# Row gathers by the sync and scalar queues: addresses as register pairs, more rows by hand, node tiles loaded singly

## Chip, core and metric

The kernel runs on one core of one Trainium2 chip. The metric is the device time of one execution in microseconds (us), as the median of several runs of the same program.

## What is computed

One layer of a graph network on 12,500 nodes with 256 features each and 200,000 edges that are sorted by their target node:

```python
h = jnp.maximum(_layernorm(x, axis=-1), 0.0)
agg = jax.ops.segment_sum(h[src], dst, num_segments=N)
z = (1.0 + eps_gin) * h + agg
t = jnp.dot(z, W1) + b1                       # 256 -> 512
t = jax.nn.relu(_batchnorm(t, g1, bt1))       # over all nodes
conv_out = jnp.dot(t, W2) + b2                # 512 -> 256
out = x + jax.nn.relu(_batchnorm(conv_out + h, g2, bt2))
```

## The kernel before, in words

**Tiles and groups.** The edges are cut into 1,563 tiles of 128 edges, the tiles into 196 groups of 8 (the last has 3). For a tile the 128 source rows of 1 KB each are fetched into SBUF, one row to a partition. TensorE multiplies them by a 128 x 96 selection matrix that VectorE makes from the target numbers, and sums the 8 tiles of a group in PSUM into a window of 96 target nodes (`aggregate`, L1324). The window is copied out, transposed (L1334) and added to `aggT` (L840). TensorE's loop has one step to a group. Every second step also brings in a node tile (128 rows of h itself, `transpose_h`, L1351), and four node tiles make a chunk that goes through W1 (`times_W1`, L1360). The chunk's result `t` is written to DRAM by `store_t` (L476). Node tile c is transposed in TensorE's step 2c + 7.

**Two phases.** Groups 0 to 29 fetch rows of x and normalise them after the fetch, since h isn't complete yet. Beside this ScalarE and VectorE normalise all of x in batches and store it as `h_rows` in DRAM. `wait_h` lets a queue go on when the last batches have landed. From group 30 on the rows are fetched from `h_rows` and used as they are; ScalarE then has no arithmetic after its step 33 until the last groups, and issues row fetches only.

**Who fetches.** Most tiles are fetched by GpSimd, with one indirect DMA of 128 rows a tile (`gather`, L650). The buffers hold four groups: group g may be fetched once group g - 4 is aggregated. Some tiles are fetched by hand, row by row: SyncE takes the last tile of the groups in `sp_groups`, ScalarE the last but one of those in `act_groups`, each with `load_rows`. A row costs a plain DMA of 1 KB whose source offset is a register. The registers are filled 32 at a time by a register load (`reg_load`, L505 on SyncE, L1191 on ScalarE) from a line of row offsets that was fetched from DRAM before (`load_at`). 16 rows are a piece, 8 pieces a tile, and each of the two engines has three row buffers: tile j may be begun when tile j - 3 has been used. GpSimd leaves these tiles out.

**How many.** `SP_EIGHTHS` counts eighths of a piece that SyncE takes in a pass. SyncE's loop has one pass for each node tile, that is for two groups, and 12 eighths are 1.5 pieces or 24 rows a pass. `ACT_EIGHTHS` counts in the same way for each of ScalarE's steps, that is for one group: 7 eighths are 14 rows. The lists of groups follow from these numbers, as in

```python
while True:
    done = ceil(8 * per_tile * (len(act_groups) + 1), ACT_EIGHTHS) + H_ACT
    if done - 1 + 4 >= NG - 4:
        break
    act_groups.append(done - 1 + 4)
```

They give SyncE 16 tiles (2 of them rows of x) and ScalarE 17, and leave 1,530 to GpSimd.

**The order on SyncE.** A pass issues, in order: the node tile's load (L460 in the first phase; in the second `load_quad`, L467, which loads four node tiles in one DMA in every fourth pass, after a wait until the four tiles that were in that buffer are transposed), every fourth pass `store_t` (it waits until the chunk's t is complete), then the rows of the pass. A DMA on this queue is issued only after all that stand before it.

Of the kernel before, what the change touches and what calls it, by code (L numbers as in the profile page):

```python
# [20 lines left out]
P = 128  # L21
D = 256
F = 512
DB, FB = D // P, F // P
GT = 8
# [11 lines left out]
XW = Q * D  # L37
X_FIRST = 4
X_EARLY = 16
SP_EIGHTHS = 12  # L40
ACT_EIGHTHS = 7
H_FROM = 30
H_NODES = 14
HB = 4
# [4 lines left out]
ROW_BUFS = 3  # L49
PIECE = 16  # L50
AT_ONCE = 32
QUAD = 4
ROW_BYTES = 4 * D


# [4 lines left out]
def build(nc, x, src, dst, W1, b1, g1, bt1, W2, b2, g2, bt2, eps_gin, out):  # L60
# [4 lines left out]
    N, E = x.shape[0], src.shape[0]  # L65

    NI = ceil(E, P * SLOTS)
    NT = ceil(N, P)
    assert NI == NT and NI >= 4 and N % 4 == 0 and NI * PG <= BANK
    LASTN = N - P * (NT - 1)  # L70
# [15 lines left out]
    with ctx:  # L86
# [3 lines left out]
        def sem(name):  # L90
            return ctx.enter_context(nc.semaphore(name))
# [4 lines left out]
        h_dram = nc.dram_tensor("h_rows", (N, D), f32, kind="Internal").ap()  # L96
# [8 lines left out]
        while True:  # L105
            done = ceil(8 * per_tile * (len(sp_groups) + 1), SP_EIGHTHS)
            if done > H_NODES or 2 * (done - 1) + 6 >= H_FROM:
# [3 lines left out]
        while True:  # L111
            done = ceil(8 * per_tile * (len(sp_groups) - SP_X + 1), SP_EIGHTHS) + H_NODES
            if 2 * (done - 1) + 6 >= NG - 4:
# [4 lines left out]
# [3 lines that stand above are left out]
# [22 lines left out]
        work, once, tables, ring = (arena[:, sum(MAIN[:n]):sum(MAIN[:n + 1])] for n in range(4))  # L143
# [6 lines left out]
                 work[:, 2 * GT * D:3 * GT * D])]  # L150
        hb = [a[:, n * 4 * D:(n + 1) * 4 * D].rearrange("p (j d) -> p j d", d=D) for a in
              (ring[:, 2 * GT * D:3 * GT * D], work[:, 2 * GT * D:3 * GT * D]) for n in (0, 1)]
        quads = [ring[:, 2 * GT * D + n * QUAD * D:2 * GT * D + (n + 1) * QUAD * D].rearrange("p (j d) -> p j d", d=D)
                 for n in (0, 1)]
        assert (NT - H_NODES) % QUAD == 0 and 2 * QUAD == GT
        after_rows = [work[:, 3 * GT * D + n * D:3 * GT * D + (n + 1) * D] for n in range(4)]
        tab_i = [work[:, n * EB * P:(n + 1) * EB * P].bitcast(i32).rearrange("p (b e) -> p b e", e=P) for n in (0, 1)]
        tab_f = [work[:, (2 + n) * EB * P:(3 + n) * EB * P].rearrange("p (b e) -> p b e", e=P) for n in (0, 1)]
# [42 lines left out]
        hx = after_rows[3]  # L201
# [68 lines left out]
        s_bn, s_mv, s_sd, s_rstd, s_st, s_h, s_sel, s_agg, s_add = (  # L270
            sem(n) for n in ("s_bn", "s_mv", "s_sd", "s_rstd", "s_st", "s_h", "s_sel", "s_agg", "s_add"))
        s_xt = [sem("s_xt_even"), sem("s_xt_odd")]
        s_quad = [sem("s_quad_even"), sem("s_quad_odd")]
        s_ev, s_wT = sem("s_ev"), sem("s_wT")
        s_xbn, s_xmv, s_xsd, s_xrs, s_xst, s_hx, s_hT, s_hTc, s_zt, s_t, s_tb, s_tst, s_td = (
            sem(n) for n in ("s_xbn", "s_xmv", "s_xsd", "s_xrs", "s_xst", "s_hx", "s_hT", "s_hTc", "s_zt",
                             "s_t", "s_tb", "s_tst", "s_td"))
# [67 lines left out]

            return a[b * QN + 4 * first:b * QN + 4 * end, :].rearrange("(p j) d -> p j d", j=4)

        NQUAD = (NT - H_NODES) // QUAD

        def quad_count(k):  # L350

            return 16 * (k // 2 + 1 + (k == NQUAD - 1))

        def quad_tile(c):

            k, j = divmod(c - H_NODES, QUAD)
            return quads[k % 2][:, j, :]

        def wait_h(eng):

# [67 lines left out]
        def _(sp):  # L428
# [7 lines left out]
            for n, a in ((1, dst), (0, src)):  # L436
                at = FULLB * P * P
# [8 lines left out]
            for a in (b1, g1, bt1, b2, g2, bt2):  # L446
                k = a.shape[0] // P
# [11 lines left out]
                    sp.wait_ge(s_hx, c - 1)  # L459
                sp.dma_start(xt[c % 2][0:n, :], x[bass.ds(c * P, n), :]).then_inc(s_xt[c % 2], 16)  # L460

            def load_quad(k):
                if k >= 2:
                    sp.wait_ge(s_hT, H_NODES + QUAD * (k - 1))
                first = H_NODES + QUAD * k
                n = QUAD if k < NQUAD - 1 else QUAD - 1
                sp.dma_start(quads[k % 2][:, 0:n, :],  # L467
                             h_dram[first * P:(first + n) * P, :].rearrange("(j p) d -> p j d", p=P)
                             ).then_inc(s_quad[k % 2], 16)
                if n < QUAD:  # L470
                    sp.dma_start(quad_tile(NT - 1)[0:LASTN, :], h_dram[N - LASTN:N, :]).then_inc(s_quad[k % 2], 16)

            def store_t(q):
                sp.wait_ge(s_tb, FB * (q + 1))
# [21 lines left out]
            def load_rows(j, m):  # L496
                if m == 0:
                    if j + 1 < len(sp_groups):
                        load_at(j + 1)
                    if j >= ROW_BUFS:  # L500
                        sp.wait_ge(s_agg, sp_groups[j - ROW_BUFS] + 1)
                    sp.wait_ge(s_spat[j % 2], 16 * (j // 2 + 1))
                if m * PIECE % AT_ONCE == 0:
                    regs = [sp.alloc_register(f"row{j}_{m}_{k}") for k in range(AT_ONCE)]
                    sp.reg_load(regs, sp_at[j % 2][0:1, m * PIECE:m * PIECE + AT_ONCE])  # L505
                    row_regs.extend(regs)
                for k in range(PIECE):
                    e = m * PIECE + k
                    reg = row_regs.pop(0)
                    at = sp.snap(reg, donate=True, min_val=0, max_val=(N - 1) * ROW_BYTES)  # L510
                    a = x_bytes if j < SP_X else h_bytes
                    sp.dma_start(sp_rows[j % ROW_BUFS][e:e + 1, :].bitcast(mybir.dt.uint8),
                                 a[bass.ds(at, ROW_BYTES)].rearrange("(p e) -> p e", p=1)
                                 ).then_inc(s_sprows[j % ROW_BUFS], 16)
                    sp.free_register(reg)

            sp.wait_ge(s_at, 1)
            sp.dma_start(at_dram.rearrange("b p e -> p b e"), tab_i[0]).then_inc(s_atd, 16)
            def pieces_of_pass(c):
# [16 lines left out]
            for c in range(NT):  # L536
                if c == NT - 1:
                    store_t(NQF - 2)
                if c < H_NODES:
                    load_node_tile(c)  # L540
                elif c == H_NODES:
                    wait_h(sp)
                    load_quad(0)
                    load_quad(1)
                elif (c - H_NODES) % QUAD == 2 and (c - H_NODES) // QUAD + 2 < NQUAD + 1:
                    k = (c - H_NODES) // QUAD + 1
                    if k >= 2:
                        load_quad(k)
                if 2 * Q < c < NT - 1 and c % Q == 1:
                    q = (c - 2 * Q - 1) // Q  # L550
                    if q == NQF - 3:
                        sp.wait_ge(s_td, 16 * q)
                        load_t(0, 0, 0)
                    store_t(q)
                if c == 0:
                    sp.wait_ge(s_trc[0], NTR)
                    sp.wait_ge(s_trc[1], NTR)
                    for b in (2, 3):
                        sp.dma_start(hb[b], batch_nodes(x, b, 0, P)).then_inc(s_pl[b], 16)
                    sp.wait_ge(s_atd, 16)  # L560
                    load_at(0)
                for j, m in pieces_of_pass(c):
                    load_rows(j, m)
# [47 lines left out]
            q, n = last_order(NQ - 1)  # L611
# [455 lines left out]
        def _(act):  # L1067
# [114 lines left out]
            def load_rows(j, m):  # L1182
                if m == 0:
                    if j + 1 < len(act_groups):
                        load_at(j + 1)
                    if j >= ROW_BUFS:
                        act.wait_ge(s_agg, act_groups[j - ROW_BUFS] + 1)
                    act.wait_ge(s_actat[j % 2], 16 * (j // 2 + 1))
                if m * PIECE % AT_ONCE == 0:
                    regs = [act.alloc_register(f"act_row{j}_{m}_{k}") for k in range(AT_ONCE)]  # L1190
                    act.reg_load(regs, act_at[j % 2][0:1, m * PIECE:m * PIECE + AT_ONCE])  # L1191
                    row_regs.extend(regs)
                for k in range(PIECE):
                    e = m * PIECE + k
                    reg = row_regs.pop(0)
                    at = act.snap(reg, donate=True, min_val=0, max_val=(N - 1) * ROW_BYTES)
                    act.dma_start(act_rows[j % ROW_BUFS][e:e + 1, :].bitcast(mybir.dt.uint8),
                                  h_bytes[bass.ds(at, ROW_BYTES)].rearrange("(p e) -> p e", p=1)
                                  ).then_inc(s_actrows[j % ROW_BUFS], 16)
                    act.free_register(reg)  # L1200
            act.wait_ge(s_atd, 16)
            load_at(0)

# [33 lines left out]
            a, c, q = NG - 4, NT - 4, NQF - 2  # L1237
# [52 lines left out]
        def _(pe):  # L1290
# [46 lines left out]
            def transpose_h(c):  # L1337
                n = P if c < NT - 1 else LASTN
                if c < H_NODES:
                    pe.wait_ge(s_hx, c + 1)  # L1340
                else:
                    k = (c - H_NODES) // QUAD
                    pe.wait_ge(s_quad[k % 2], quad_count(k))
                h = hx if c < H_NODES else quad_tile(c)
                if 1 <= c < NT - 1:
                    pe.wait_ge(s_hTc, c)
                if c == NT - 1:
                    pe.wait_ge(s_sel, NG)
                hT = hT_ps if c < NT - 1 else hT_last
                for f in range(DB):  # L1350
                    last = T.transpose(hT[:, f, 0:n], h[0:n, f * P:(f + 1) * P], ident[0:n, 0:n])  # L1351
                last.then_inc(s_hT, 1)
# [40 lines left out]
            a, c, q = NG - 4, NT - 4, NQF - 2  # L1393
# [90 lines left out]
```

## Time and profile before

| | |
|---|---|
| median of 3 runs | 2143.56 us (2143.31 to 2145.06) |
| the profiled execution: its own time | 2143.43 us |
| its span in the profile | 2141.6 us |
| GpSimd gathers (L650) | 16 + 222 + 1292 = 1530 |
| GpSimd issues gathers from / to | 3.8 us / 1916.5 us |
| granted TensorE clock, mean | 0.83 |

The span is the time from the first to the last instruction that the profiler saw. Times of single instructions are in ns, stretches in us from the span's start. PE is TensorE, DVE is VectorE, ACT is ScalarE, POOL is GpSimd, SP is SyncE; SPq and ACTq are the DMA issues of these engines. Register loads and moves and DMA issues are not counted as busy time of an engine.

### The profile page before, as it was taken

How to read it: one execution, taken by the hardware profiler on the slowest of the kernel's cores; microseconds unless marked ns; L12 is line 12 of the kernel's file. 1: busy time of each engine (PE TensorE's matmuls, PEld its weight loads, DVE VectorE, ACT ScalarE, POOL GpSimd, SP SyncE). 2: the span in 40 equal slices, each digit the busy share in tenths (PEclk: the TensorE clock that was granted, in tenths of full speed). 3: DMA queues.
4: the chain of work that ended last, by engine and by line, in shares of the span. 5: the costliest groups of instructions: out<-in, count | busy, mean ns of one | idle time of the engine just before them, and what ended most of it. 6: DMA issues, size and time to landing. Idle time of an engine off the chain costs nothing.

```text
span 2141.6 us, 24025 instructions
## 1 busy us (share of the span) xinstructions
PE 1430.6 (67%) x4835; PEld 911.2 (43%) x4835; DVE 768.3 (36%) x1947; ACT 338.3 (16%) x661; POOL 1449.2 (68%) x1540
## 2 busy tenths in 40 slices
PE   3656666665655766675666566666666666689998
PEld 2434344443433434343444334434344444454446
DVE  7777753222322222322232222222232232234447
ACT  6767660000000000000000000000000000014446
POOL 7777777777777777777777777777777777760000
PEclk7788788877888787888888887778787788899999
DMA  6666654444434434444444443443443444448438
GB/s 200 214 224 218 225 175 129 132 117 139 138 108 139 138 110 136 137 118 130 136 126 119 138 139 108 138 137 107 140 137 108 136 135 123 137 133 321 176 135 319
DMA packets 123554, 325.22 MB, mean 152 GB/s; under 512 B 32179, under 2 KB 55294, under 8 KB 117266
## 3 DMA queue, kind: packets, MB, share of 16 engines
q0 software_dynamic: 73440, 200.64, 32.0%
q1 hardware_dynamic: 39100, 97.34, 12.8%
q10 hardware_dynamic: 10870, 25.75, 3.6%
q8 instruction: 38, 0.62, 0.1%
q14 instruction: 106, 0.87, 0.1%
HBM read 271.55 MB, written 52.05 MB: 151 GB/s over the span
## 4 chain that ended last, share of the span: by engine, by line
POOL 65%; issue 21%; PE 12%; DMA 2%; ACT 0%; DVE 0%; SPq 0%; POOLq 0%; DVEq 0%
POOL arena L650 65%; PE ps L1442 8%; PE ps L1324 2%; PE ps L1456 2%; DMA arena<-h_rows,arena 1%; PE ps L1360 0%; PE ps L1398 0%; DMA arena<-in_src 0%; ACT aggT L1072 0%; SPq L439 0%; ACT arena L1078 0%; ACT arena L1076 0%; DVE arena L1057 0%; PE ps L1334 0%; SPq L433 0%
## 5 line engine op out<-in xcount | busy, mean ns | idle before, releaser
L650 POOL DMA_INDIRECT arena<-h_rows,arena x1292 | 1221.6, 946 | 394.0 <-issue 391.5
L1324 PE MATMUL ps<-arena 128*96 128x256 f32 x3060 | 976.9, 489 | 675.2 <-DMA arena<-h_rows,arena 561.5
L1324 PEld LDWEIGHTS ps<-arena 128*96 128x96 f32 x3060 | 640.8, 216 | 993.3 <-issue 732.4
L840 DVE TENSOR_TENSOR aggT<-aggT,ps 128x192 f32 x196 | 69.3, 353 | 1074.2 <-PE ps L1334 1071.2
L1151 ACT COPY arena<-ps 96x256 f32<-96x256 f32 x37 | 13.2, 357 | 1575.5 <-PE ps L1334 1545.0
L650 POOL DMA_INDIRECT arena<-in_x,arena x222 | 209.9, 946 | 67.7 <-issue 67.7
L1360 PE MATMUL ps<-arena 128*128 128x512 f32 (+3 forms) x412 | 186.3, 577 | 1.6 <-DVE arena L873 1.5
L1442 PE MATMUL ps<-arena,W2s 128*128 128x512 f32 (+1 forms) x400 | 168.1, 582 | 0.9 <-ACT arena L1272 0.8
L927 DVE TENSOR_TENSOR arena<-arena,ps 128x768 f32<-128x768 f32 x159 | 149.8, 942 | 0.0
L1103 ACT ACTIVATE arena<-arena,nb,mv 128x256 f32<-128x256 f32 x238 | 120.2, 587 | 83.6 <-DVE nb L744 81.5
L1442 PEld LDWEIGHTS ps<-arena,W2s 128*128 128x128 f32 x400 | 75.7, 190 | 93.2 <-issue 86.3
L676 DVE BATCH_NORM_STATS2 st<-arena 128x6 f32<-128x256 f32 x238 | 80.5, 410 | 61.5 <-DMA arena<-in_x,arena 61.4
L1360 PEld LDWEIGHTS ps<-arena 128*128 128x128 f32 x412 | 69.7, 190 | 48.1 <-issue 44.5
L1272 ACT ACTIVATE arena<-arena,sh,sc 128x512 f32<-128x512 f32 (+1 forms) x100 | 72.1, 792 | 90.2 <-PE ps L1442 80.3
L924 DVE TENSOR_SCALAR arena<-ps,prmT 128x512 f32<-128x512 f32 x79 | 59.3, 751 | 73.7 <-PE ps L1360 73.7
L1035 DVE SCALAR_TENSOR_TENSOR aggT<-ps,prmT,aggT 128x512 f32<-128x512 f32 (+1 forms) x50 | 36.9, 738 | 95.7 <-PE ps L1442 95.7
L881 DVE BATCH_NORM_STATS2 arena<-arena 128x6 f32<-128x512 f32 x92 | 62.9, 684 | 10.3 <-ACT arena L1160 10.3
L1334 PEld LDWEIGHTS ps<-ident,arena 96*128 96x128 f32 x392 | 55.3, 142 | 26.5 <-ACT arena L1151 1.2
L918 DVE COPY arena<-ps 96x256 f32<-96x256 f32 x159 | 65.8, 414 | 0.1
L1334 PE MATMUL ps<-ident,arena 96*128 96x96 f32 x392 | 64.9, 246 | 0.6 <-ACT arena L1151 0.5
L1117 ACT ACTIVATE arena<-arena,pnb,pmv 128x256 f32<-128x256 f32 (+1 forms) x100 | 51.7, 591 | 0.0
L756 DVE TENSOR_TENSOR arena<-arena,ps 128x768 f32<-128x768 f32 x37 | 35.0, 945 | 8.7 <-PE ps L1324 8.7
(99 smaller groups left out, 575.2 us busy)
## 6 DMA issues: line engine op xcount, KB each, us to landing
W2s<-h_rows ACTq DMA_DIRECT2D x2176, 1.0 KB
rl_odd<-h_rows SPq DMA_DIRECT2D x1792, 1.0 KB
t_T<-arena SPq DMA_DIRECT2D x24, 1024.0 KB, 4.9
arena<-t_T SPq DMA_DIRECT2D x24, 1024.0 KB, 4.8
arena<-h_rows,arena POOLq DMA_INDIRECT x1292, 2.8
arena<-in_x SPq DMA_DIRECT2D x27, 512.0 KB, 5.7
h_rows<-arena ACTq DMA_DIRECT2D x24, 512.0 KB, 3.4
out<-arena SPq DMA_DIRECT2D x23, 512.0 KB
```

The source lines that it names most:

```text
L650: nc.gpsimd.indirect_dma_start(out=rows[slot(g)][:, k, :], out_offset=None, in_=(x if g < H_FROM else h_dram)[:, :], in_offset=bass.Indire ...
L676: last = V.bn_stats(o, r)
L840: V.tensor_tensor(z, z, winT_ps, ALU.add).then_inc(s_add, 1)
L881: V.bn_stats(o, t[:, m, :]).then_inc(s_tst, 1)
L918: V.tensor_copy(win_sb[g % 2], win_ps[g % 2]).then_inc(s_ev, 1)
L927: V.tensor_tensor(sel[:, g % 2, :, :], rel[:, g * GT:(g + 1) * GT].unsqueeze(2).to_broadcast([P, GT, W]), iota_ps.unsqueeze(1).to_broadcas ...
L1103: last = S.activation(rows_of(g, k), rows_of(g, k), ACT.Relu, bias=nb[:, g % 2, k:k + 1], scale=mv[:, g % 2, k, 1:2])
L1272: S.activation(u[:, k % 2, f, 0:n], tin[:, k % 2, f, 0:n], ACT.Relu, bias=sh1[:, f:f + 1], scale=sc1[:, f:f + 1]).then_inc(s_u, 1)
L1324: last = T.matmul(win_ps[g % 2], sel[:, g % 2, k, :], rows_of(g, k), start=k == 0, stop=k == n - 1)
L1334: last = T.transpose(winT_ps[:, f, :], win_sb[w % 2][:, f * P:(f + 1) * P], ident[0:W, 0:W])
L1360: last = T.matmul(t_ps[(FB * q + m) % TB][:, a:b], W1s[:, k, m * P:(m + 1) * P], zt[q % 2][:, k, a:b], start=k == 0, stop=k == DB - 1)
L1442: last = T.matmul(c_ps[k % 2][m][:, 0:n], W2s[:, f, m * P:(m + 1) * P], u[:, k % 2, f, 0:n], start=f == 0, stop=f == FB - 1)
```

## The change

Three things change together. The row's address is given as a pair of registers, the offset and a register that holds zero for the upper half, in place of the offset alone. SyncE takes 44 rows a pass in place of 24, ScalarE 22 rows a group in place of 14. And in the second phase each node tile is loaded by a DMA of its own, three passes ahead (four in pass 14), into a ring of eight buffers, in place of four tiles in a DMA.

```diff
-SP_EIGHTHS = 12
-ACT_EIGHTHS = 7
+SP_EIGHTHS = 22
+ACT_EIGHTHS = 11
...
-QUAD = 4
+NODE_BUFS = 8
+NODES_AHEAD = 4
...
-            def load_quad(k):
-                if k >= 2:
-                    sp.wait_ge(s_hT, H_NODES + QUAD * (k - 1))
-                first = H_NODES + QUAD * k
-                n = QUAD if k < NQUAD - 1 else QUAD - 1
-                sp.dma_start(quads[k % 2][:, 0:n, :],
-                             h_dram[first * P:(first + n) * P, :].rearrange("(j p) d -> p j d", p=P)
-                             ).then_inc(s_quad[k % 2], 16)
...
+            def load_node_rows(c):
+                n = P if c < NT - 1 else LASTN
+                if c - NODE_BUFS >= H_NODES:
+                    sp.wait_ge(s_hT, c - NODE_BUFS + 1)
+                sp.dma_start(node_tile(c)[0:n, :], h_dram[c * P:c * P + n, :]
+                             ).then_inc(s_node[(c - H_NODES) % NODE_BUFS], 16)
...
-                    at = sp.snap(reg, donate=True, min_val=0, max_val=(N - 1) * ROW_BYTES)
+                    at = sp.snap(bass.Register64Pair(reg, no_high), donate=True, min_val=0,
+                                 max_val=(N - 1) * ROW_BYTES)
...
+            no_high = sp.alloc_register("no_high")
+            sp.reg_mov(no_high, 0)
...
                 elif c == H_NODES:
                     wait_h(sp)
-                    load_quad(0)
-                    load_quad(1)
-                elif (c - H_NODES) % QUAD == 2 and (c - H_NODES) // QUAD + 2 < NQUAD + 1:
-                    k = (c - H_NODES) // QUAD + 1
-                    if k >= 2:
-                        load_quad(k)
+                    for n in range(NODES_AHEAD):
+                        load_node_rows(c + n)
+                elif c + NODES_AHEAD - 1 < NT:
+                    load_node_rows(c + NODES_AHEAD - 1)
...
-                    at = act.snap(reg, donate=True, min_val=0, max_val=(N - 1) * ROW_BYTES)
+                    at = act.snap(bass.Register64Pair(reg, no_high), donate=True, min_val=0,
+                                 max_val=(N - 1) * ROW_BYTES)
```

TensorE's `transpose_h` waits for the node tile's own semaphore in place of the quad's.

## Rows read from the trace of the kernel before

**Rows 1.** The page: busy time by engine (GpSimd's line), and the chain that ended last.

```profile
PE 1430.6 (67%) x4835; PEld 911.2 (43%) x4835; DVE 768.3 (36%) x1947; ACT 338.3 (16%) x661; POOL 1449.2 (68%) x1540
POOL 65%; issue 21%; PE 12%; DMA 2%; ACT 0%; DVE 0%; SPq 0%; POOLq 0%; DVEq 0%
```

**Rows 2.** Groups of instructions: busy us, mean ns of one, idle before with its releasers.

```profile
L650 POOL DMA_INDIRECT arena<-h_rows,arena x1292 | 1221.6, 946 | 394.0 <-issue 391.5 <-PE ps L1324 2.4
L1324 PE MATMUL ps<-arena 128*96 128x256 f32 x3060 | 976.9, 489 | 675.2 <-DMA arena<-h_rows,arena 561.5 <-ACT arena L1103 101.0 <-ACT rl_odd L1103 6.8
```

**Rows 3.** Line L650 over the span: ns min/median/max, first and last start.

```profile
L650 POOL DMA_INDIRECT arena<-h_rows,arena x1292: 942/946/1005, 302.2 to 1916.5; - x185
L650 POOL DMA_INDIRECT arena<-in_x,arena x222: 942/946/969, 24.6 to 300.9; - x111
```

**Rows 4.** Row issues and register loads, by line: ns min/median/max.

```profile
L512 SPq MOVE rl_odd<-h_rows x1792: 29/29/29, 298.7 to 1742.0; - x200
L512 SPq DMA_DIRECT2D rl_odd<-h_rows x1792: 227/228/532, 298.8 to 1742.1; - x200
...
L1197 ACTq DMA_DIRECT2D W2s<-h_rows x2176: 234/235/1232, 316.6 to 1638.8; - x198
...
L505 SPq TENSOR_LOAD <-rl_odd x64: 2032/2132/4272, 24.5 to 1699.7; - x64
...
L1191 ACTq TENSOR_LOAD <-W2s x68: 2136/2245/4123, 314.3 to 1626.1; - x68
```

**Rows 5.** Timeline of SyncE's queue, 950 to 1050 us: start, length, what.

```profile
957.79 0.40 SPq L467 DMA_DIRECT2D arena<-h_rows  x1
...
964.29 0.36 SPq L476 DMA_DIRECT2D t_T<-arena  x1
...
994.75 5.17 SPq L512 DMA_DIRECT2D rl_odd<-h_rows  x16
1035.39 0.41 SPq L467 DMA_DIRECT2D arena<-h_rows  x1
```

**Rows 6.** Timeline of SyncE's queue at the start: two issues without a move between.

```profile
7.42 0.25 SPq L448 DMA_DIRECT2D arena<-in_L_gnn_b  x1
7.72 0.25 SPq L448 DMA_DIRECT2D arena<-in_L_gnn_g  x1
```

**Rows 7.** Timeline of ScalarE's queue, 870 to 1012 us.

```profile
876.29 51.64 ACTq L1197 DMA_DIRECT2D W2s<-h_rows  x128
...
963.84 48.27 ACTq L1197 DMA_DIRECT2D W2s<-h_rows  x118
```

**Rows 8.** Waits of SyncE's queue: us in total, times, longest.

```profile
SPq L467 <- PE ps L1351: 630.7, 19, 64.0
SPq L476 <- DVE arena L924: 126.5, 20, 20.2
```

**Rows 9.** DMA queues, 1065 to 1083 us: packets, MB, share of 16 engines.

```profile
q0 software_dynamic: 678, 1.86, 36.5%
q1 hardware_dynamic: 87, 0.05, 1.1%
q10 hardware_dynamic: 89, 0.05, 1.0%
...
W2s<-h_rows ACTq DMA_DIRECT2D x48, 1.0 KB
```

**Rows 10.** Line L650, 1065 to 1083 us.

```profile
L650 POOL DMA_INDIRECT arena<-h_rows,arena x15: 942/946/949, 1065.0 to 1082.5; - x15
```

**Rows 11.** Timeline of TensorE after the change of phase.

```profile
318.15 3.67 PE L1324 MATMUL ps<-arena 128*96 128x256 f32 x16
...
343.89 3.66 PE L1324 MATMUL ps<-arena 128*96 128x256 f32 x16 [2.33 <-DMA arena<-h_rows,arena]
```

**Rows 12.** Timeline of SyncE's queue in the first phase.

```profile
61.49 0.37 SPq L460 DMA_DIRECT2D arena<-in_x  x1
61.95 14.53 SPq L512 DMA_DIRECT2D rl_odd<-in_x  x32
```

More of the change, by code:

```diff
@@ L152, in build @@
               (ring[:, 2 * GT * D:3 * GT * D], work[:, 2 * GT * D:3 * GT * D]) for n in (0, 1)]
-        quads = [ring[:, 2 * GT * D + n * QUAD * D:2 * GT * D + (n + 1) * QUAD * D].rearrange("p (j d) -> p j d", d=D)
-                 for n in (0, 1)]
-        assert (NT - H_NODES) % QUAD == 0 and 2 * QUAD == GT
+        node_rows = ring[:, 2 * GT * D:3 * GT * D].rearrange("p (j d) -> p j d", d=D)
+        assert NODE_BUFS == GT
         after_rows = [work[:, 3 * GT * D + n * D:3 * GT * D + (n + 1) * D] for n in range(4)]
@@ L272, in build @@
         s_xt = [sem("s_xt_even"), sem("s_xt_odd")]
-        s_quad = [sem("s_quad_even"), sem("s_quad_odd")]
+        s_node = [sem(f"s_node{b}") for b in range(NODE_BUFS)]
         s_ev, s_wT = sem("s_ev"), sem("s_wT")
@@ L346, in batch_nodes, with node_tile, node_count @@
             return a[b * QN + 4 * first:b * QN + 4 * end, :].rearrange("(p j) d -> p j d", j=4)
[L348 to L357, printed above, removed]
+        def node_tile(c):
+            return node_rows[:, (c - H_NODES) % NODE_BUFS, :]
+        def node_count(c):
+            return 16 * ((c - H_NODES) // NODE_BUFS + 1)
         def wait_h(eng):
@@ L460, in load_node_tile @@
                 sp.dma_start(xt[c % 2][0:n, :], x[bass.ds(c * P, n), :]).then_inc(s_xt[c % 2], 16)
-            def load_quad(k):
-                if k >= 2:
-                    sp.wait_ge(s_hT, H_NODES + QUAD * (k - 1))
-                first = H_NODES + QUAD * k
-                n = QUAD if k < NQUAD - 1 else QUAD - 1
-                sp.dma_start(quads[k % 2][:, 0:n, :],
-                             h_dram[first * P:(first + n) * P, :].rearrange("(j p) d -> p j d", p=P)
-                             ).then_inc(s_quad[k % 2], 16)
-                if n < QUAD:
-                    sp.dma_start(quad_tile(NT - 1)[0:LASTN, :], h_dram[N - LASTN:N, :]).then_inc(s_quad[k % 2], 16)
+            def load_node_rows(c):
[4 more added lines that the diff above has]
+                             ).then_inc(s_node[(c - H_NODES) % NODE_BUFS], 16)
             def store_t(q):
@@ L1200, in load_rows @@
                     act.free_register(reg)
+            no_high = act.alloc_register("act_no_high")
+            act.reg_mov(no_high, 0)
             act.wait_ge(s_atd, 16)
@@ L1341, in transpose_h @@
                 else:
-                    k = (c - H_NODES) // QUAD
-                    pe.wait_ge(s_quad[k % 2], quad_count(k))
-                h = hx if c < H_NODES else quad_tile(c)
+                    pe.wait_ge(s_node[(c - H_NODES) % NODE_BUFS], node_count(c))
+                h = hx if c < H_NODES else node_tile(c)
                 if 1 <= c < NT - 1:
```

## The prediction

> **What bounds the kernel now.** I read the page first. No engine is busy for more than 68% of the span, so the shares alone don't name a bound. The chain that ended last does: 65% of the span is GpSimd's gather line and 21% is "issue", which is GpSimd's own gap between two gathers [rows 1]. The reader is to see that these two are one thing. The groups of instructions confirm it: before its 1,292 gathers of h rows GpSimd idles 394.0 us, and all but 2.4 us of that is "issue", not a wait for anybody [rows 2]. TensorE on its side idles 675.2 us before the aggregation, and 561.5 us of it end with the landing of a gather [rows 2]. So GpSimd never waits, and the others wait for it.
>
> Its pace comes from first and last starts. From 302.2 to 1916.5 us lie 1,291 intervals, 1614.3 / 1291 = 1.250 us each; from 24.6 to 300.9 us lie 221, again 1.250 us [rows 3]. A gather costs 1.25 us in both phases, with everything that happens beside it. The time before the first gather and the work after the last are not touched by the change.
>
> **What the change takes off GpSimd.** The lists of groups follow from the two numbers. SyncE's h tiles end in pass 14 + ceil(64 n / 22) and so on up to the last group below 192; I count 4 tiles of x (2 before) and 27 of h (14 before), the last for group 190. ScalarE gets 27 (17 before), the last also for group 190. That is 58 tiles in place of 33, so GpSimd keeps 1,505 of 1,563: 25 fewer, 2 of them in the first phase. 25 x 1.250 = 31.3 us. This is the whole gain if SyncE and ScalarE have their rows ready in time and GpSimd keeps its pace. The rest of this part is about that "if".
>
> **What a row costs the issuing queues.** Today a row is a move of 29 ns and a DMA issue of 228 ns on SyncE (235 ns on ScalarE) [rows 4]. Sixteen rows take 5.17 us from the first start to the last end, so a period is (5.17 - 0.23) / 15 = 0.33 us, 0.322 if the first, slower one is left out; 0.322 - 0.228 - 0.029 leaves 0.065 us for two gaps [rows 4, 5]. The move fills the upper half of the address. I take it that the pair does away with it, which saves 0.029 + 0.032 = 0.061 us: 0.261 us a row on SyncE and 0.264 on ScalarE. The bounds: nothing saved (0.322), if a second issue must follow the first no sooner than now. The nearest rows without a move between are two small loads at the start, 0.30 us from start to start with 0.25 us of issue [rows 6]; by their gap of 0.05 a row would take 0.28. I stay with 0.261, as the row's own issue and gap are seen 1,792 times.
>
> **ScalarE's budget.** A tile of 128 rows takes it 51.64 us [rows 7] plus the register load ahead of the first row, 2.25 us [rows 4]: 53.9 us with all its loads. Less 128 x 0.061 = 7.8 it is 46.1 us. After the change a group of the second phase has 8 - 2 x 22/128 = 7.66 gathers, 9.57 us, and ScalarE must deliver a tile in 128/22 = 5.82 groups, 55.7 us. It has 9.6 us to spare, and still 1.8 us if nothing is saved.
>
> **SyncE's budget.** Four passes take it from 957.79 to 994.75 + 5.17 = 999.92, 42.1 us, for 96 rows, one quad, one `store_t` and three register loads, one of them right behind the store [rows 5]. Afterwards four passes hold 176 rows: 80 more are 25.8 us at today's period, 2.5 more register loads of 2.13 us [rows 4] are 5.3, three more node loads of 0.41 us and a gap [rows 5] 1.4, the more frequent row-offset loads 0.2; the saved moves give back 176 x 0.061 = 10.7. Sum 64.1 us, 16.0 a pass. Four passes of GpSimd are 8 x 9.57 = 76.6 us. Spare: 12.5 us, or 1.8 if nothing is saved.
>
> **The node tiles.** Today SyncE waits 630.7 us in 19 quad loads, up to 64.0 us each [rows 8]: it does four passes in 42 us, then stands until four node tiles are used. With 64 us of work in each 76.6 these bursts would leave little cover; loading singly, a pass c waits only for tile c - 5 to be transposed, so SyncE may run five passes ahead. What holds it then is `store_t`, which waits for t today too (126.5 us in 20 waits, [rows 8]): it can be issued in TensorE's step 8q + 18 for chunk q, and VectorE needs it done by step 8q + 23. SyncE arrives there ahead, so nothing behind it is late: the rows queued behind the store are due at step 8q + 24. I cost the ring at nothing; the cover is these five steps, some 48 us. Without it each late microsecond would be one of the end.
>
> **The first phase.** SyncE's first tile is now for group 10, in passes 0 to 2. Pass 1 starts at 61.5 us, and 32 rows of x took it 14.5 us [rows 12]. With 48 rows in it and in pass 2 the tile is issued by about 61.5 + 19 + 18 = 99 us. GpSimd's seventh gather of group 10 is the 71st of those that start at 24.6 us, thus at 24.6 + 70 x 1.25 = 112 us [rows 3]. Cost nothing, cover 13 us.
>
> **The change of phase.** In its steps 29 to 32 ScalarE has row pieces ahead of its window copies: 5 in place of 3, with one more register load. 32 x 0.264 + 2.2 - 48 x 0.061 = 7.7 us later. TensorE has a backlog there: from 318.15 to 343.89 us it goes through four groups in 25.7 us and only then waits for a gather again [rows 11], where GpSimd needs 40 us for four. The 14 us hide the 7.7. Without this cover they would be added whole.
>
> **DMA engines.** With both row streams running beside GpSimd, its own queue takes 36.5% of 16 engines, the rows 1.1% and 1.0% for 43 and 45 rows in 18 us [rows 9]. The worst case is that all rows go through one engine. It then spends 2.1% x 16 = 34% on them, 36.5% on gathers, 70% in all; at 0.26 us a row 34 becomes 42, together 78%. So no engine is full. GpSimd's gathers in that stretch still start 17.5 / 14 = 1.25 us apart [rows 10]. [...]
>
> **Sum.** 2143.43 - 31.3 = 2112.2 us against the profiled execution's own time; the median is 0.13 above that, so 2112.3.
>
> **The rivals.**
> *Start-up leaks.* The 7.7 us of the change of phase reach GpSimd through its four group buffers: 2112.3 + 7.7 = 2120. Against it the backlog above; for it that the buffers' slack in the first phase is under a group. 6%.
> *Rows become the bound (the other side).* If the pair costs a second move instead of saving one, a row on ScalarE takes 0.386 us and a tile 53.9 + 7.8 = 61.7. ScalarE starts at about 310 us (316.6 today, [rows 4], with a piece in one step earlier) and would end 27 tiles at 310 + 27 x 61.7 = 1976. Group 190's gathers are issued today 43 gathers before the last, by 1916.5 - 53.8 = 1862.7. So 113 us slower: 2257. It turns slower than before once a tile costs over (1862.7 - 310) / 27 = 57.5 us, a row over 0.264 + 11.4 / 128 = 0.353. For it: I haven't seen the instructions of a pair. Against: only a rise over today's 0.325 can do it. 4%.
> *Issues take turns.* SyncE's and ScalarE's issues could exclude one another, 0.228 + 0.235 = 0.463 us for a pair of rows. Then four passes of SyncE take 64.1 + 176 x 0.202 = 99.7 us, 27 tiles of 2.91 passes end at 299 + 78.5 x 24.9 = 2254, 391 us past 1862.7: 2535. Against it: 43 + 45 rows went out in 18 us beside register loads, where turns allow 39 pairs [rows 9], and both medians are those of a lone issue [rows 4]. 1%. The Trainium skill ("Perfetto Trace Analysis", section "DMA Instruction — HWDGE (DVE, Sync)") has the rule: a descriptor generator shared by the sequencers and locked by one at a time. The trace doesn't agree at this rate.
> *GpSimd slows down.* More row traffic lengthens each gather. Break-even is 31.3 / 1505 = 21 ns, 1.271 us a gather; half of that gives 2128. Against it the equal pace in both phases and in rows 10. 4%.
> *The pair saves nothing.* Both budgets keep 1.8 us: still 2112, part of the forecast.
>
> **How the numbers follow.** The forecast has 85%, with its own range 2110 to 2116. The range to state reaches below to 2109 (half a gather's noise and a slightly earlier start of phase two) and above over the start-up case and small losses, to 2122; what lies outside is the row bound, the turns and a slowed GpSimd, about 1 in 10. A change under 0.2% (4.3 us) can't be told from none. Faster: forecast, start-up and half of the slowed-GpSimd case, 0.92. Same 0.03, slower 0.05.
>
> **What would show it.** In the profile after: 1,505 gathers, still 946 ns and 1.25 us apart; the last one starts near 1916.5 - 31.3 = 1885 us; no MOVE at the row line and 16 rows in about 4.2 us; ScalarE's 128 rows in 44 us; quad waits of 630 us gone, a few waits of `load_node_rows` and longer ones of `store_t` in their place; TensorE waits for gathers, not for `rl_odd` or `W2s` rows. Wrong would be: GpSimd waiting for TensorE over more than some us, TensorE's idle time ended by row DMAs, or gathers further apart.

## The result: slower by 1.1%, and the profile after

The changed kernel takes 2167.77 us (2166.18 to 2169.39) against 2143.43 us in the same comparison: ratio 1.0112, 95% interval 1.0095 to 1.013. The forecast was 2112.3 us. The span of the profiled execution is 2165.6 us (2141.6 before).

The gathers first, line L644 of the changed kernel; they answer to [rows 2] and [rows 3].

```profile
L644 POOL DMA_INDIRECT arena<-h_rows,arena x1269: 942/946/963, 300.2 to 1940.3; - x182
L644 POOL DMA_INDIRECT arena<-in_x,arena x220: 942/946/957, 24.2 to 299.0; - x110
```

With 16 more at the start there are 1,505 of them, each still 946 ns. The last one starts at 1940.3 us, where the forecast had 1885: 55 us late, and 55 us are all that is missing (2167.8 - 2112.3). The waits of the changed kernel say why (engine, line, what it waited for; us in total, times, longest):

```profile
POOL arena L644 <- issue: 452.8, 1484, 0.3
PE ps L1321 <- DMA arena<-h_rows,arena: 321.4, 74, 9.0
DVE arena L918 <- DMA t_T<-arena: 279.8, 15, 37.2
PE ps L1321 <- DMA rl_odd<-h_rows: 174.2, 15, 21.6
...
PE ps L1321 <- DVE arena L921: 88.4, 9, 24.0
...
POOL arena L644 <- PE ps L1321: 60.8, 18, 9.1
```

GpSimd now waits 60.8 us for TensorE to free its buffers, where it waited 2.4 before. TensorE waits 174.2 us for `rl_odd`, which is SyncE's rows, and VectorE 279.8 us for the store of t, which stands in the same queue. That second wait reaches TensorE too: it waits 88.4 us for the selection matrices (L921), which VectorE makes behind the copy that the store holds up; in the kernel before this was 1.5 us. ScalarE's rows (`W2s`) end none of these waits. The chain that ended last has changed hands; the issues of SyncE's queue, 0% of it in [rows 1], are now 35%:

```profile
SPq 35%; POOL 29%; issue 17%; PE 14%; DMA 3%; DVE 0%; ACT 0%; DVEq 0%; POOLq 0%
```

So SyncE's queue is late. Its row line, to be read against [rows 4], and its waits against [rows 8]:

```profile
L506 SPq MOVE rl_odd<-h_rows x3456: 29/29/29, 298.4 to 1893.9; - x192
L506 SPq DMA_DIRECT2D rl_odd<-h_rows x3456: 227/228/2461, 298.5 to 1893.9; - x192
```

```profile
SPq L469 <- ACT arena L1154: 27.9, 1, 27.9
...
SPq L469 <- DVE arena L918: 3.7, 2, 3.1
```

Two things stand there. The move of 29 ns is still in front of each of the 3,456 rows. And the longest issue is 2,461 ns where it was 532, though the median is the same 228. SyncE itself hardly waits any more: for t 3.7 us in place of 126.5, and once, after 1800 us, 27.9 us for the last t that ScalarE makes (73.7 before); there are no quad waits. The timeline of its queue over four passes answers to [rows 5]:

```profile
1424.65 0.48 SPq L463 DMA_DIRECT2D arena<-h_rows  x1
1425.19 0.42 SPq L469 DMA_DIRECT2D t_T<-arena  x1
1425.71 7.32 SPq L506 DMA_DIRECT2D rl_odd<-h_rows  x16
...
1467.73 18.86 SPq L506 DMA_DIRECT2D rl_odd<-h_rows  x48
...
1487.10 5.64 SPq L506 DMA_DIRECT2D rl_odd<-h_rows  x16
...
1507.67 0.36 SPq L463 DMA_DIRECT2D arena<-h_rows  x1
```

From node load to node load these are 1507.67 - 1424.65 = 83.0 us for four passes without a wait, where GpSimd needs 76.6. Sixteen rows take 5.64 to 7.32 us here, 5.17 in [rows 5]. Over the 14 such stretches between 502 and 1671 us the mean is 83.5.

### The profile page after: what moved, and what is told of

Same layout as the page of the kernel before. It is cut to its first block, busy times and chain, and to the rows that moved or that the text cites. A ratio compares the mean times of both kernels' runs of the same rounds, so it can differ in the third digit from the quotient of the medians.

```text
span 2165.6 us, 30624 instructions
## 1 busy us (share of the span) xinstructions
PE 1367.9 (63%) x4835; PEld 882.2 (41%) x4835; DVE 765.9 (35%) x1947; ACT 338.5 (16%) x661; POOL 1425.0 (66%) x1515
## 4 chain that ended last, share of the span: by engine, by line
SPq 35%; POOL 29%; issue 17%; PE 14%; DMA 3%; DVE 0%; ACT 0%; DVEq 0%; POOLq 0%
POOL arena L644 29%; SPq L506 28%; PE ps L1438 8%; SPq L498 6%; PE ps L1321 3%; DMA rl_odd<-h_rows 2%; PE ps L1452 1%; DMA arena<-h_rows,arena 1%; PE ps L1356 1%; SPq L463 1%; SPq L485 0%; SPq L469 0%; PE ps L1394 0%; ACT arena L1097 0%; PE ps L1331 0%
## 5 line engine op out<-in xcount | busy, mean ns | idle before, releaser
L644 POOL DMA_INDIRECT arena<-h_rows,arena x1269 | 1199.7, 945 | 441.6 <-issue 382.0
L1321 PE MATMUL ps<-arena 128*96 128x256 f32 x3010 | 909.0, 468 | 760.4 <-DMA arena<-h_rows,arena 321.4
L1321 PEld LDWEIGHTS ps<-arena 128*96 128x96 f32 x3010 | 603.2, 206 | 1041.3 <-issue 800.1
L644 POOL DMA_INDIRECT arena<-in_x,arena x220 | 208.0, 945 | 68.0 <-issue 66.8
L918 DVE TENSOR_SCALAR arena<-ps,prmT 128x512 f32<-128x512 f32 x79 | 59.1, 749 | 328.4 <-DMA t_T<-arena 279.8
L921 DVE TENSOR_TENSOR arena<-arena,ps 128x768 f32<-128x768 f32 x159 | 149.7, 942 | 0.0
L1438 PEld LDWEIGHTS ps<-arena,W2s 128*128 128x128 f32 x400 | 75.8, 190 | 93.1 <-issue 86.2
L1347 PE MATMUL ps<-ident,arena 128*128 128x128 f32 x196 | 37.3, 272 | 2.3 <-ACT aggT L1138 2.3
```

The source lines that it names most:

```text
L644: nc.gpsimd.indirect_dma_start(out=rows[slot(g)][:, k, :], out_offset=None, in_=(x if g < H_FROM else h_dram)[:, :], in_offset=bass.Indire ...
L921: V.tensor_tensor(sel[:, g % 2, :, :], rel[:, g * GT:(g + 1) * GT].unsqueeze(2).to_broadcast([P, GT, W]), iota_ps.unsqueeze(1).to_broadcas ...
L1321: last = T.matmul(win_ps[g % 2], sel[:, g % 2, k, :], rows_of(g, k), start=k == 0, stop=k == n - 1)
L1438: last = T.matmul(c_ps[k % 2][m][:, 0:n], W2s[:, f, m * P:(m + 1) * P], u[:, k % 2, f, 0:n], start=f == 0, stop=f == FB - 1)
```

## The experiments

Theory A: the rows of both queues overfill something that they share, a DMA engine. Theory B: SyncE simply has too much work of its own. Theory C: the address pairs or the single node loads did it. The runs came in series, each with the kernel before beside it. In four series that kernel took 2570 to 2611 us; their times stand in the last part. The kernel with other row shapes ran in one of those four, which is said there. In the other series the kernel before took 2143.8 to 2144.0 us.

**The counts of before, the rest of the change kept.**

```diff
-SP_EIGHTHS = 22
-ACT_EIGHTHS = 11
+SP_EIGHTHS = 12
+ACT_EIGHTHS = 7
```

> The changed kernel with the row counts of before (12 and 7 eighths): only the address pairs and the node tiles loaded one by one remain of the change. GpSimd has 1,530 gathers again. Theory A (one DMA engine or the issue path is overfilled by rows) and theory B (SyncE alone has more work than a pass of GpSimd's lasts) both expect 2143 us, within 0.2%, as 52 rows a pass leave room in either. If the single node loads themselves are the cause (63 more DMAs in SyncE's queue, theory C), it is slower than before by over 0.2%. The move of 29 ns in front of each row should still be there, as in the changed kernel.

Measured: 2143.40 us, ratio 1.000 (0.999 to 1.001). The pairs and the single loads together cost and bring nothing at these counts. The pair doesn't take the move away:

```profile
L506 SPq MOVE rl_odd<-h_rows x1792: 29/29/29, 299.7 to 1709.9; - x200
```

**One queue's rows as after, the other's as before** (12 and 11 eighths, then 22 and 7).

> The changed kernel with SyncE's rows as before (12 eighths, 24 rows a pass) and ScalarE's as after (11 eighths, 44 rows a pass): 68 rows in two groups in place of 88, 1,520 gathers. If nothing binds but GpSimd: 2143.4 - 10 x 1.25 = 2130.9. Theory A expects about that, 2130 to 2134, with ScalarE's row issues near 235 ns, since the rows of both queues together are 23% fewer. Theory B expects the same. A theory that ScalarE's rows are the late ones expects over 2140.

Measured: 2131.23 us, ratio 0.9941 (0.9925 to 0.9958).

> The changed kernel with SyncE's rows as after (22 eighths, 44 a pass) and ScalarE's as before (7 eighths, 28 a pass): 72 rows in two groups, 1,515 gathers. If nothing binds but GpSimd: 2143.4 - 15 x 1.25 = 2124.7. Theory A (what the two queues share is full) expects 2124 to 2130 and SyncE's mean row issue back from 273 to under 240 ns, since ScalarE's part is smaller. Theory B (SyncE's own work, whatever ScalarE does) expects SyncE to be as late as in the changed kernel: row issues of 270 ns and a time of 2155 to 2168.

Measured: 2125.89 us, ratio 0.9914 (0.9898 to 0.9931). Theory B falls: the same 44 rows a pass are in time when ScalarE issues 28 beside them and not when it issues 44. Four passes of SyncE in this run:

```profile
1419.80 0.36 SPq L463 DMA_DIRECT2D arena<-h_rows  x1
1422.80 0.35 SPq L469 DMA_DIRECT2D t_T<-arena  x1
1427.71 17.70 SPq L506 DMA_DIRECT2D rl_odd<-h_rows  x48
...
1497.76 0.36 SPq L463 DMA_DIRECT2D arena<-h_rows  x1
```

78.0 us, and 2.6 of them are a wait for t ahead of the store: 75.4 us of work. In the changed kernel the same rows, node loads and store take 83.0, although only five register loads (10.4 us) fall into them and six here (14.6 us, one of them behind the store). The row issues make the difference: 230 ns each in this stretch, 294 in the changed kernel's. A run of 48 rows with one register load is 17.70 us here, 18.86 above, and up to 22.02 elsewhere in the changed kernel:

```profile
1095.94 22.02 SPq L506 DMA_DIRECT2D rl_odd<-h_rows  x48
```

**A row's cost by itself.** A kernel that leaves the whole layer out, copies x to the output and issues rows with constant addresses.

```python
for e in range(R):                                        # R = 256, on ScalarE and on SyncE
    act.dma_start(place(act_rows, e), row(e, 1)).then_inc(s_a[1], 16)
act.wait_ge(s_a[1], FULL)
```

> Not the layer: the output is a copy of x, and beside it rows of x are fetched to measure what a row costs. Addresses are constants, so no move and no register load stand between issues. Stage 1: ScalarE alone 256 rows. Stage 2: both queues 256 each. Stage 3: the same beside 48 gathers of GpSimd. Stages 4 and 5: as 2 and 3, but each row cut into 16 pieces of 64 bytes. Theory A with all rows on one DMA engine: stage 1 is issue bound, 0.26 us a row; stage 2 is bound by the engine, 512 rows in 512 x c us, where the changed kernel suggests c of 0.12 to 0.14 us: 61 to 72 us, against 68 us of pure issue, and the issues stretch beyond 235 ns once some 30 rows a queue are outstanding; stage 3 takes about 1/(1 - 0.37) as long, 100 to 115 us. If the cost is a fixed one per row and engine, the cut rows of stages 4 and 5 take as long as the whole ones or longer; if it is bytes, they take less. Theory B expects stages 2 and 3 to stay at 0.26 us a row and queue, 68 us each. GpSimd's gathers should stay 1.25 us apart in stage 3 by both.

Three of its five stages: ScalarE alone issues 256 rows, then both queues 256 each, then both again, with 48 gathers of GpSimd beside the first 60 us. The timeline of both queues, and behind it SyncE's waits for the landing after stages 2 and 3:

```profile
42.80 75.96 ACTq L42 DMA_DIRECT2D act_rows<-in_x  x256
119.77 77.81 ACTq L45 DMA_DIRECT2D act_rows<-in_x  x256
119.83 77.93 SPq L73 DMA_DIRECT2D sp_rows<-in_x  x256
211.97 85.09 SPq L77 DMA_DIRECT2D sp_rows<-in_x  x256
212.03 85.16 ACTq L49 DMA_DIRECT2D act_rows<-in_x  x256
```

```profile
SPq L80 <- DMA act_rows<-in_x: 17.2, 1, 17.2
...
SPq L75 <- DMA act_rows<-in_x: 14.0, 1, 14.0
```

Alone a row takes 75.96 / 256 = 0.297 us to issue, without any move. Two queues issue as fast (0.304), so they don't take turns. But the rows don't land as fast: 77.9 + 14.0 = 91.9 us for 512 rows, 0.180 us each, and 85.1 + 17.2 = 102.3 us, 0.200 each, in the stage with gathers. Theory A expected 61 to 72 us for the first, so a row costs more than the 0.12 to 0.14 us it supposed; the second lies in its 100 to 115. Theory B had 68 us for each. GpSimd's gathers stayed 1.25 us apart. The DMA queues of stage 2, 120 to 197 us (packets, MB, share of 16 engines):

```profile
q1 hardware_dynamic: 440, 0.23, 3.2%
q10 hardware_dynamic: 441, 0.23, 3.0%
```

In stage 1 ScalarE's rows landed as fast as they were issued: to the last one a row's packet started 0.6 to 0.7 us after its issue. In stage 2 that delay grew to 11.7 us. So both queues share something that lets a row pass every 0.18 us. That it is one DMA engine fits but isn't shown by the packets' time: 6.2% of 16 engines is 99% of one, but with rows of 256 bytes (next part) the same sum is 9.8%, or 157% of one, so a packet's time holds some waiting too. What speaks for one engine is the count of packets. A row goes out as one piece and leaves two, one of 1 KB and one of 4 bytes (440 for 220 rows); a row in 16 pieces leaves 16 of each. The Trainium skill ("DMA: Bandwidth & Descriptors", section "Why a DMA increments its semaphore by 16 and not by 1") says that the outermost dimension above 1, as the instruction carries it, decides how many engines a DMA uses, that a [1, 1] scalar uses one, that on these two queues it is always the lowest-numbered ones, and that each engine taking part writes once to the semaphore. The trace agrees with the count; which engine it is can't be seen. Beside gathers, 213 to 272 us:

```profile
q0 software_dynamic: 2193, 5.99, 36.6%
q1 hardware_dynamic: 293, 0.15, 1.6%
q10 hardware_dynamic: 293, 0.15, 1.3%
```

That is 293 rows in 59 us, two packets each, 0.201 us a row: the limit next to gathers, though by packet time the engine would be only 36.6 + 2.9 x 16 = 83% busy. So the packets' time is no measure of what a row costs: too little here, too much at 256 bytes. Stages 4 and 5, with the row cut into 16 pieces that lie together, came out like 2 and 3 (77.95 and 84.37 us of issue) and still sent two packets a row, so the cut had been merged and says nothing.

**Does the size of a row matter?** The same kind of kernel, layer left out, both queues issuing 256 DMAs in each of five stages: whole rows, 256 bytes of each, rows in 4 and in 16 pieces, and two rows (2 KB) in one DMA. It ran in a series where the kernel before took 2611 us; its first stage repeats the 77.9 us of the row kernel, so its issues were not slowed.

```diff
+act.dma_start(whole(act_rows, e, D // 4), row(e, 1, D // 4)).then_inc(s_a[1], 16)      # 256 bytes
+act.dma_start(apart(act_rows, e, 4), pieces(e, 2, 4)).then_inc(s_a[2], 16)             # 4 pieces apart
+act.dma_start(apart(act_rows, e, 16), pieces(e, 3, 16)).then_inc(s_a[3], 16)           # 16 pieces apart
```

> Not the layer: the output is a copy of x. Five stages, in each both queues fetch 256 rows at once with constant addresses and wait until all have landed. Stage 1: whole rows of 1 KB, as measured before, 0.175 us a row from first issue to last packet (89.5 us for 512). Stage 2: 256 bytes of each row. Stage 3: a row in 4 pieces of 256 bytes that don't lie together in SBUF, stage 4 in 16 pieces of 64 bytes, stage 5: two rows, 2 KB, in one DMA. Fixed cost per DMA on its engine: stage 2 and 5 take 85 to 95 us as well, and stages 3 and 4 too, as each engine that takes part pays it. Cost by bytes: stage 2 becomes issue bound (76 us), stage 5 takes 130 us or more, stages 3 and 4 become issue bound as the load is spread over 4 and 16 engines.

The timeline of SyncE's queue, by stage:

```profile
42.62 77.92 SPq L71 DMA_DIRECT2D sp_rows<-in_x  x256
136.54 76.07 SPq L75 DMA_DIRECT2D sp_rows<-in_x  x256
229.77 187.93 SPq L79 DMA_DIRECT2D sp_rows<-in_x  x256
419.51 164.70 SPq L83 DMA_DIRECT2D sp_rows<-in_x  x256
585.45 80.06 SPq L87 DMA_DIRECT2D sp_rows<-in_x  x256
```

With the waits for the landing behind them (15.9, 17.0, 1.7, 0.9 and 14.2 us) 512 DMAs take 93.8 us at 1 KB, 93.1 at 256 bytes and 94.3 at 2 KB. The cost is fixed per DMA, 0.18 us, as expected. The forms in pieces were expected at 85 to 95 us if each engine pays, and missed that: they do not queue up, but their issue takes 0.73 and 0.64 us, far over the 0.30 of a whole row, so cutting a row into pieces is no way out. The DMA queues at 256 bytes, 137 to 226 us:

```profile
q10 hardware_dynamic: 512, 0.07, 6.8%
q1 hardware_dynamic: 512, 0.07, 3.0%
```

**Between the two counts** (18 and 10 eighths, 20 and 10, 20 and 11).

> The changed kernel with 18 and 10 eighths, 76 rows in two groups, 1,514 gathers. 2123.4 if nothing but GpSimd binds, and Theory A expects 2123 to 2125, row issues of SyncE under 245 ns. An effect in proportion to the row count would give about 2155.

> The changed kernel with 20 and 10 eighths, 80 rows in two groups, 1,512 gathers. 2120.9 if nothing but GpSimd binds. Theory A: 80 x 0.204 + 1 = 17.3 us in 19.2, 90% full, so 2121 to 2124, the fastest of this series or level with 84 rows.

> The changed kernel with 20 and 11 eighths, 84 rows in two groups, 1,509 gathers. 2117.2 if nothing but GpSimd binds. Theory A: 17.1 + 1 us of work for the row engine in 19.2 us, 95% full: 2117 to 2130; at such a load the queues behind it should be long (row issues over 240 ns in the mean).

Measured: 2124.51 us (ratio 0.9904, 0.9887 to 0.992), 2120.97 (0.989, 0.9873 to 0.9906) and 2117.89 (0.9875, 0.9859 to 0.9891). All three stand within 1.1 us of what GpSimd's gathers alone give; only the guess that 80 rows would be the fastest or level was off. The last is the fastest version found, 26 us faster than before and 50 faster than the changed kernel. GpSimd waits for TensorE 2.7 us or less in each. The step from 84 to 88 rows, all four of them SyncE's, costs 50 us.

**The same 84 rows, but more of them on SyncE** (22 and 10 eighths).

> The changed kernel with 22 and 10 eighths for the third time, again because the chip before took 2600 us for the kernel before. Theory A (the number of rows on the one engine decides): 2116 to 2119, like 20 and 11. Theory D (SyncE's own work and what its issues lose to the full engine, together): 2135 to 2160.

Measured: 2127.95 us, ratio 0.9924 (0.9907 to 0.9941). This lies between the two expectations: 12 us over the 2115.9 of its gathers, where 20 and 11 is 0.7 over. The total number of rows alone (theory A) doesn't decide; SyncE's own 44 rows do count. Theory D, both together (SyncE's own work and what its issues lose), has the right sign and too large a size. It is again SyncE that is late:

```profile
PE ps L1321 <- DMA rl_odd<-h_rows: 91.9, 12, 13.8
POOL arena L644 <- PE ps L1321: 13.8, 5, 5.8
```

**Counts of after, nothing else of the change** (the kernel before with 22 and 11 eighths: no pairs, node tiles in fours).

> Once more the kernel before with the counts of after (22 and 11 eighths), without pairs and single node loads, since the chip of the last series took 2610 us for the kernel before and can't settle it. Theory A (the DMA engine that carries all rows is full at 88 rows in two groups): 2165 us or more, up to 2200 if the four-tile loads cost SyncE more. Theory C (pairs or single loads made the changed kernel slow): near 2112.

Measured: 2157.87 us, ratio 1.0061 (1.0044 to 1.0078). Its gathers alone would give 2112.2, so the counts by themselves lose 46 of the 55.6 us that are missing. Theory C, which expected 2112, falls, and so does my expectation of 2165 us or more. With pairs and single loads it is 10 us slower still. GpSimd waits 50.8 us for TensorE here.

**The queue in front of the engine.** From the packets of the traces I took, for each of ScalarE's rows, the time from the end of its issue to the start of its packet, and the mean length of SyncE's row issues, both from 400 to 1700 us of each run:

```
eighths      rows in     gathers   time by gathers   measured   SyncE's row   from issue to packet,
(SP, ACT)    2 groups              alone, us         us         issue, ns     median / 95%, us
12,  7 before   52        1530        2143.4         2143.4       231.7         1.1 /  2.9
12, 11          68        1520        2130.9         2131.2       231.3         1.1 /  3.1
22,  7          72        1515        2124.7         2125.9       238.4         2.6 / 10.2
18, 10          76        1514        2123.4         2124.5       235.7         2.3 /  5.4
20, 10          80        1512        2120.9         2121.0       242.0         8.0 / 11.5
20, 11          84        1509        2117.2         2117.9       264.3        10.6 / 12.7
22, 10          84        1508        2115.9         2128.0       266.2         9.8 / 12.2
22, 11 after    88        1505        2112.2         2167.8       281.3        10.8 / 12.7
22, 11 fours    88        1505        2112.2         2157.9       278.0        11.4 / 14.0
```

Before, a row's packet starts a microsecond after its issue. From 80 rows on it starts 8 to 11 us after, and hardly more than that (95% of them within 14): the queue is then as long as it gets, and the issues stretch instead. In the second stage of the kernel that measured rows alone the same was seen: ScalarE's issues stayed at 265 to 273 ns until the delay had grown to 11 us, and then took 316 to 320.

**The series in which the kernel before took 2570 to 2611 us.**

> The kernel before with the row counts of after (22 and 11 eighths) and nothing else of the change: no address pairs, node tiles in fours. 88 rows in two groups, 1,505 gathers. Theory A (the one DMA engine that carries all rows is full at 88 rows): at least as slow as the changed kernel, 2165 us or more, and slower still if the waits of the four-tile loads cost SyncE time that it no longer has, up to 2200. Theory C (the pairs or the single loads made the changed kernel slow, not the counts): near 2112.

> The changed kernel with 20 eighths on SyncE and 11 on ScalarE: 84 rows in two groups, 1,509 gathers, 2117.2 if nothing but GpSimd binds. Theory A with 0.204 us a row beside gathers (measured in the row kernel): 84 x 0.204 = 17.1 us and about 1 us of other traffic in 19.2 us, 95% full: 2117 to 2125. At 88 rows it was 99%. Theory B (SyncE's own work alone): 40 rows a pass are 9% less than 44, so also about 2117.

> The changed kernel with 18 eighths on SyncE and 10 on ScalarE: 76 rows in two groups, 1,514 gathers, 2123.4 if nothing but GpSimd binds. Theory A: 76 x 0.204 + 1 = 16.5 us in 19.3, 86% full, so 2123 to 2125, and faster than before by 0.9%. If a linear effect of row traffic on everything is at work instead of a threshold, it lies between 2143 and 2168, near 2155.

> The changed kernel with 22 and 10 eighths: SyncE's 44 rows a pass as after, ScalarE's 40: 84 rows in two groups, as in the run with 20 and 11, and 1,508 gathers, 2115.9 if nothing but GpSimd binds. If the number of rows on the one engine is what decides (theory A), this is like 20 and 11: 2116 to 2119. If what decides is SyncE's own work of 18.7 us a pass plus what its issues lose to the full engine (1.7 us at 38 ns a row, theory D: both together), SyncE needs 20.4 us of 19.2 and is late as in the changed kernel: 2135 to 2160.

> The changed kernel with 21 and 11 eighths: 42 and 44 rows, 86 in two groups, 1,508 gathers, 2115.9 if nothing but GpSimd binds. Theory D: SyncE needs 17.9 + 1.8 = 19.7 us a pass of 19.2; the excess of 0.5 over 78 passes is 39 us, about what its head start of some 37 us covers (it is in front until 970 us in the changed kernel at 1.06 us of excess a pass): 2116 to 2125. Theory A: 18.5 us of 19.2 on the engine, 97% full: 2116 to 2140.

> The kernel before with 20 and 11 eighths, node tiles still in fours and no pairs: 84 rows in two groups, 1,509 gathers. With single loads it took 2117.9. If the single loads only cost SyncE issue time (0.9 us in four passes more than the fours), this is the same or up to 1 us faster: 2116.5 to 2118.5. If the fours' waits (until four tiles are used, up to 64 us in the kernel before) leave SyncE too little of a head start at 40 rows a pass, it is slower: 2125 to 2145. This is what the single loads were worth.

> Once more the changed kernel with 22 and 10 eighths, as the chip of the last series took 2572 us for the kernel before. 84 rows in two groups, 1,508 gathers, 2115.9 if nothing but GpSimd binds. Theory A (the number of rows on the one engine decides): 2116 to 2119, like 20 and 11. Theory D (SyncE's own work and what its issues lose to the full engine, together): SyncE needs 20.4 us a pass of 19.2 and is late: 2135 to 2160.

> The kernel before with 20 and 11 eighths, node tiles still in fours and no pairs: 84 rows in two groups, 1,509 gathers, 2117.2 if nothing but GpSimd binds; with single loads it took 2117.9. If the single loads only cost SyncE issue time: 2116.5 to 2118.5. If the fours' waits leave SyncE too little of a head start at 40 rows a pass: 2125 to 2145; this is what the single loads were worth.

Against a kernel before of 2570 to 2611 us these took, as ratios: 18 and 10 eighths 1.128, 20 and 11 1.171, 21 and 11 1.185, 22 and 10 1.216 and 1.219, 22 and 11 with fours 1.222, 20 and 11 with fours 1.164 and 1.165. None of their expectations can be judged by times. ScalarE's row line in the first run with 22 and 10 shows what was different there:

```profile
L1192 ACTq MOVE W2s<-h_rows x3072: 2/29/1396, 434.3 to 2616.7; - x192
```

A move of 29 ns takes up to 1.4 us (342 of these 3,072 take over 0.1 us, and these 0.68 in the mean), so the queues that do much by hand are slowed; why, no run shows. The order of the ratios follows SyncE's share. The run with 21 and 11 eighths and the one with fours at 84 rows have no counterpart in the other series, so what the single loads are worth at 84 rows stays open.

## Why the prediction was wrong

**Right:** GpSimd's pace and the count of gathers. All nine versions of the table, from 1,505 to 1,530 gathers, issue a gather every 1.25 us where they don't wait, and six of them, the kernel before among them, came out within 1.2 us of gathers times pace. The start was right too: group 10's rows are issued by 103.4 us (99 predicted), and the first gather of h starts at 300.2 us, 2.0 us earlier. The change of phase leaks nothing to GpSimd; until 960 us it waits 1.9 us for TensorE, and the first wait of some length stands at 972. Two rivals fell: issues don't take turns, and gathers don't slow down.

**The step that failed first: "I take it that the pair does away with it", with the move of 29 ns.** It doesn't; 3,456 rows still have 3,456 moves, so the reason I gave ("The move fills the upper half of the address") isn't borne out; what the move does no run shows. Even without a move a row takes 0.297 us to issue by the row kernel, not 0.261, so the gap behind an issue can't be read from one that has a move behind it; the small loads at the start of the trace, 0.30 us apart [rows 6], were the better row, and I had passed them over. By my own sum for this case ("if nothing is saved") SyncE needed 64.1 + 10.7 = 74.8 us of 76.6 in four passes. The run with 22 and 7 shows 75.4, so this sum was sound to 0.6 us and SyncE had a spare of 1 to 2 us, where I had counted on 12.5. The same step took ScalarE's spare: in the changed kernel it begins a tile of 128 rows every 55.0 us (median), where I had 46.1 and it may take 55.7. By the prediction's own sums this step alone would have left the forecast standing: it is the rival "The pair saves nothing", with 1.8 us to spare.

**The step that decided: "So no engine is full".** I took the right case, all rows through one engine, and sized it by the packets' time: 2.1% x 16 for 88 rows in 18 us, 0.07 us a row. The measured cost is 0.18 us a DMA whatever its size and 0.20 beside gathers, nearly three times as much. With it 88 rows need 17.7 us of 19.1, 92%, before node tiles and t are counted. By packet time they need 32% in the mean, and with the gathers' 36.5% that is 68% (the 78% of the prediction is for stretches in which both queues issue). From 80 rows on a row's packet starts 8 to 11 us after its issue; the delay grows no further, and the issuing instructions pay. I had put nothing for that. SyncE's row issue went from 238 ns with 72 rows to 281 with 88: 43 ns on 176 rows are 7.6 us in four passes, and 75.4 + 7.6 = 83.0 against the 83.5 measured in the mean. This is 6 to 7 us over GpSimd's 76.6. SyncE lived on its head start until 970 us, then came TensorE's waits for `rl_odd`.

**"I cost the ring at nothing".** The single loads did give SyncE freedom from the quad waits, but it had no time left to use it. Where SyncE is the late one, three more issues in four passes are paid: the run with fours is 10 us faster. This reading of the 10 us is argued from the count of issues; no run isolates it from the address pairs, which also changed. The cover of `store_t` went with the same lateness (279.8 us of VectorE's waits); how much of the 55 us is due to the store and how much to the rows wasn't separated, both stand in one queue. TensorE's two waits, 174.2 us for rows and 88.4 for VectorE, show that both reach it.

**The rival that came nearest** is the one that the rows become the bound, with 4%. Its mechanism was another: a second move, with ScalarE as the late queue. Its threshold of 0.353 us a row was for ScalarE, and doesn't carry over. For SyncE the prediction's own sum leaves 76.6 - 18.1 = 58.5 us for 176 rows, 0.332 us each, and SyncE's row now takes 0.281 + 0.09 = 0.37 us in the mean. That figure could have been worked out beforehand: today's 0.322 was already within 0.01 us of it.

## What to carry to other kernels

Single-row DMAs from SyncE and ScalarE share one limit: here both queues together landed one in 0.18 to 0.20 us whatever its size, at 256 bytes to 2 KB. Count DMAs against such a limit, not bytes and not the packets' busy time. A budget that two queues keep only to within a few per cent is no budget: of 88 rows in two groups, four fewer on SyncE gave 50 us, four fewer on ScalarE 40. Where one engine is the bound and others relieve it by hand, move the share in small steps and stop where the late engine first waits for nothing.

## What the runs showed of the hardware that I had not expected

- The two queues together land single-row DMAs at 0.18 us each, at 256 bytes, 1 KB and 2 KB alike (93.1, 93.8 and 94.3 us for 512), and at 0.20 us beside gathers, while a row's packets are busy for 0.07 us in the kernel before.
- When a row's packet starts 8 to 11 us after its issue, the issuing instruction slows down: in the changed kernel up to 2.5 us for one issue and 281 ns in the mean, while the median stays at 228 ns.
- A pair of registers as address has the same move in front as a single register.
- On some chips the kernel before took 2570 to 2611 us in place of 2143. In the run with 22 and 10 eighths there, moves of 29 ns took up to 1.4 us, while a gather kept 949 ns.
